# A token-by-token scan: the product of decays moved to GpSimd, one sum reordered, one scaling done a group later

## The chip, the core and the metric

The kernel runs on one core of one Trainium2 chip, in one launch. The metric is the device time of that launch in microseconds (us), read as the median of several runs. A core has five engines with instruction queues of their own: TensorE (PE in the profile), VectorE (DVE), ScalarE (ACT), GpSimd (POOL) and SyncE (SP, which only issues DMAs here). They meet through semaphores: an instruction waits until a counter has reached a value and raises a counter when it is done.

## What is computed

The whole kernel is a stack of four attention-like parts and four feed-forward parts on an input of 8 x 256 x 256. The change touches one part only, the last "attention", which is in truth a recurrence over the 256 tokens of each batch entry (x stands for the normalised input, the context gives the first weights):

```python
lr = 1.0 / X.shape[-1]
def step(W, x_t):
    pre = jnp.einsum('boi,bi->bo', W, x_t)
    y_t = jax.nn.sigmoid(pre)
    dW = jnp.einsum('bo,bi->boi', y_t, x_t) - (y_t ** 2)[..., None] * W
    W_new = W + lr * dW
    return (W_new, y_t)
_, m_traj = lax.scan(step, W_init, jnp.swapaxes(X, 0, 1))
```

Each output row o of W is multiplied at each token by the decay 1 - lr * y_t(o)^2 and gets lr * y_t(o) * x_t added. So pre for a later token s can be carried forward without W: v[s] begins as W_init x_s, and at each token t it becomes v[s] * (1 - lr * y_t^2) + lr * y_t * (x_t . x_s). The inner products x_t . x_s (the "gram") are made ahead of the scan by TensorE.

## The kernel before, in words

`stage_scan` runs `scan_products` (grams and first products), `scan_steps` (the recurrence) and `stage_tail` (the last feed-forward part). The change is in `scan_steps` alone.

A tile holds 128 rows of the output dimension in its partitions and C = 16 columns for (half of the output dimension, batch entry). 256 tokens are walked in NG = 64 groups of TG = 4; four groups make a block of TB = 16. At token t = 4m + i VectorE brings up to date only what lies near: the rest of group m and all of group m + 1. What older groups add to later tokens goes through TensorE, a group at a time: for each group the kernel keeps a = the product of its decays so far (slot 0 of tile `az`) and y of each token, decayed by the tokens behind it in the group (slots 1 to 4). When the group is over, z = y decayed / a (`ra` is the reciprocal of a), TensorE turns z (`ps_z`), ScalarE copies it (`zT`), and TensorE adds its products with the gram to an accumulator in PSUM (`acc`). Two tokens before group m + 1 begins, that accumulator times the running a is the share of all older groups (`far`), and is added to v.

Order of VectorE's queue in one token, with the widths in elements per partition (16 a token):

- `adds` (line 2956): y_t times the gram for the tokens ahead, 48, 96, 80, 64 wide at i = 0, 1, 2, 3.
- `left` for the next token (line 2962): v of it times the decay; the decay comes as nq = -lr * y^2 (line 2971), and (nq + 1) * v is one instruction. 16 wide, 64 at i = 3.
- `az` (line 2962 through 2986 or 2991): a and the y's of this group times the decay, in place, 16, 32, 48, 64 wide.
- v of the next token = `adds` + `left` (line 2993), which waits for `left`. ScalarE waits for this v, makes y by a sigmoid (line 2930), and then a second copy of y for `az` (line 2934).
- `left` for the rest of the tokens ahead, and their sum (line 3036). At i = 0 one more product starts v of the group after (line 2956).
- At i = 2 the rest goes otherwise: `left` (3004), `far` (3008), `left` + `adds` (3012), nq of the next token, and v = `left` + `far` (3017).
- At i = 3: the reciprocal (3025) and z (3030).
- nq of the next token (2971), which waits for ScalarE's y.

ScalarE copies zT of group m - 1 in its queue behind the sigmoids of token 4m + 1 (i = 1), after a wait for TensorE's `z_ps`. TensorE, in each group, waits for z, turns it, does one early piece of work, waits for zT, adds the group's products (which raises `acc_ready`), does a share of products of whole older blocks, and fills up with matmuls on an identity (`ss_idle`, line 3081) until the group has PASSES = 28 passes. GpSimd has no instruction in `scan_steps`.

`step()` in the code raises VectorE's own counter `own`; several waits ahead of one instruction are put on it (the first) and on semaphore instructions ahead of it (the others).

Of the kernel before, what the change touches and what calls it, by code (L numbers as in the profile page):

```python
# [12 lines left out]
P = 128  # L13
# [14 lines left out]
KD = D // P  # L28
# [2843 lines left out]
def scan_steps(nc, core, gd, band, p0, gm, gb, first_in, y_all, LR, TB, TG):  # L2872
# [5 lines left out]
    PASSES = 28  # L2878
    QUARTER = (0, 1, 0, 1, 2, 3, 0, 1, 0, 1, 2, 3, 0, 1, 2, 3)
    with ExitStack() as ctx:  # L2880
        st = Stage(nc, ctx, "ss")
        v = st.sb("v", [P, C, S])
        nq = st.sb("nq", [P, 2, C])
# [3 lines left out]
        az = st.sb("az", [P, 2, C, 1 + TG])  # L2887
# [8 lines left out]
        v_ready, y_ready, yz_ready, z_ready = (st.sem(n) for n in ("v_ready", "y_ready", "yz_ready", "z_ready"))  # L2896
        z_ps, zT_ready, acc_ready, merged = (st.sem(n) for n in ("z_ps", "zT_ready", "acc_ready", "merged"))
# [26 lines left out]
        @block.scalar  # L2924
        def _(act):
            nc.scalar.preload_act_table(ACT.Sigmoid)
            for t in range(S):
                m, i = divmod(t, TG)
                act.wait_ge(v_ready, t + 1)
                nc.scalar.activation(y_all[:, :, :, t], by_batch(v[:, :, t]), ACT.Sigmoid).then_inc(y_ready, 1)  # L2930
                if m < SENT:
                    if i == 0 and m >= 2:
                        act.wait_ge(z_ready, m - 1)
                    nc.scalar.activation(az[:, m % 2, :, 1 + i], v[:, :, t], ACT.Sigmoid).then_inc(yz_ready, 1)
                if i == 1 and 0 < m <= SENT:
                    k, g = divmod(m - 1, PER)
                    rows = slice(32 * g, 32 * (g + 1))
                    act.wait_ge(z_ps, m)
                    nc.scalar.activation(zT[rows, k, :, :].rearrange("p h n -> p (h n)"),
                                         ps_z[(m - 1) % 2][rows, 0:KD * P], ACT.Copy).then_inc(zT_ready, 1)  # L2940

        @block.vector
        def _(dve):
# [16 lines left out]
            def decayed(out, t, src, n):  # L2960

                return nc.vector.scalar_tensor_tensor(  # L2962
                    out, nq[:, t % 2, :].unsqueeze(2).broadcast_to([P, C, n]), 1.0, src, ALU.add, ALU.mult)

            nq_done, summed = {}, [0]

            def square(t):

                yt = y_all[:, :, :, t]
                dve.wait_ge(y_ready, t + 1)  # L2970
                nq_done[t] = step(nc.vector.scalar_tensor_tensor(by_batch(nq[:, t % 2, :]), yt, -LR, yt,
                                                                 ALU.mult, ALU.mult))

            def token(t):
# [9 lines left out]
                if m < NG - 1:  # L2984
                    if i == 0:
                        a_done = step(decayed(az[:, m % 2, :, 0:1], t, az[:, 1 - m % 2, :, 0:1], 1))
                    else:
                        n = 1 + i if m < SENT else 1
                        if n > 1:
                            dve.wait_ge(yz_ready, t)  # L2990
                        a_done = step(decayed(az[:, m % 2, :, 0:n], t, az[:, m % 2, :, 0:n], n))
# [3 lines left out]
                cols = slice(t + 1 + first, t + 1 + old)  # L2995
                if i == 2 and m < NG - 1:
# [7 lines left out]
                    left_done = step(decayed(lft[:, :, first:old], t, v[:, :, cols], old - first))  # L3004
                    if m > 0:
                        dve.wait_ge(acc_ready, m)
                    dve.wait_ge(own, a_done)
                    nc.vector.tensor_tensor(by_batch(far[:, :, :]), past,
                                            by_batch(az[:, m % 2, :, 0:1]).broadcast_to([P, KD, B, TG]), ALU.mult
                                            ).then_inc(merged, 1)  # L3010
                    dve.wait_ge(own, left_done)
                    left_done = step(nc.vector.tensor_tensor(lft[:, :, first:old], lft[:, :, first:old],
                                                             add[:, :, first:old], ALU.add))
                    square(t + 1)
                    dve.wait_ge(merged, m + 1)
                    dve.wait_ge(own, left_done)
                    summed[0] = step(nc.vector.tensor_tensor(v[:, :, cols], lft[:, :, first:old], far[:, :, :], ALU.add))
# [5 lines left out]
                if i == TG - 1 and m < SENT:  # L3023
                    dve.wait_ge(own, a_done)
                    ra_done = step(nc.vector.reciprocal(ra[:, :], az[:, m % 2, :, 0]))
                    dve.wait_ge(own, ra_done)
                    dve.wait_ge(yz_ready, t + 1)
                    if m >= 2:
                        dve.wait_ge(z_ps, m - 1)
                    nc.vector.tensor_tensor(z[:, m % 2, :, :, :].rearrange("p h i b -> p h b i"),  # L3030
                                            by_batch(az[:, m % 2, :, 1:1 + TG]),
                                            by_batch(ra[:, :].unsqueeze(2)).broadcast_to([P, KD, B, TG]), ALU.mult
                                            ).then_inc(z_ready, 1)
# [6 lines left out]
            step(nc.vector.memset(az[:, 1, :, 0:1], 1.0))  # L3040
            nc.vector.tensor_copy(by_batch(v[:, :, 0:TG]), p0[:, :, :, 0:TG]).then_inc(v_ready, 1)
            square(0)
            for t in range(S - 1):
# [6 lines left out]
                token(t)  # L3050

# [422 lines left out]
```

## Time and profile before

| what | value |
| --- | --- |
| median of 3 runs | 2093.52 us (2092.69 to 2096.36) |
| profiled execution, its own time | 2117.26 us |
| its span, first to last instruction | 2115.4 us |
| the scan's tokens in it | about 1741 to 2021 us of the span |
| busy over the whole span: PE, DVE, ACT, POOL | 89%, 60%, 39%, 13% |
| mean granted TensorE clock | 0.942 of full |

The profile is one execution, recorded with every instruction's start and duration in each engine. An instruction of VectorE may start before the one ahead of it has ended, so that sums of durations exceed the time they take; the distance from start to start is what an instruction costs its queue. Idle time ahead of an instruction is shown in brackets with the instruction that ended it.

### The profile page before, as it was taken

The numbers are of one execution on the slowest core, as the hardware profiler recorded it, in microseconds if no ns is written. First come the engines' busy times: TensorE is split into PE (matmuls) and PEld (weight loads), VectorE is DVE, ScalarE is ACT, GpSimd is POOL, SyncE is SP. The second block draws the span as 40 slices with busy tenths as digits, with TensorE's granted clock in tenths as the row PEclk, the third lists the DMA queues.
The fourth block names the chain that finished last, engine by engine and source line by source line (L and its number), as shares of the span: only waits on it lengthen the run. The fifth ranks groups of instructions, "written<-read, shape, count | busy, mean of one in ns | idle before, by whom it ended". The sixth has DMA issues, their size and how long they took to land. (4 is left out here: it accounts for less than half of the span.)

```text
span 2115.4 us, 39004 instructions
## 1 busy us (share of the span) xinstructions
PE 1874.4 (89%) x13651; PEld 1515.8 (72%) x13652; DVE 1270.9 (60%) x4667; ACT 835.4 (39%) x2279; POOL 275.6 (13%) x499
## 2 busy tenths in 40 slices
PE   8799997999998989999999988997940969999978
PEld 6466765667666979999999977775520857777745
DVE  7767764887784351111111144676778518999988
ACT  3333334565563111111111102773477523444468
POOL 2001112000001070000000063430000230000022
PEclk9899998999999999999999998998975987999989
DMA  6111112111112622222222021111000030111101
GB/s 220 65 45 56 55 53 75 41 66 55 41 41 61 237 80 80 82 85 84 82 84 84 25 68 38 48 41 61 0 0 1 0 102 23 35 36 47 25 8 33
DMA packets 106722, 124.95 MB, mean 59 GB/s; under 512 B 36160, under 2 KB 85832, under 8 KB 104776
## 3 DMA queue, kind: packets, MB, share of 16 engines
q1 hardware_dynamic: 95416, 107.25, 15.3%
q0 software_dynamic: 3072, 8.39, 1.3%
q10 hardware_dynamic: 8080, 7.35, 1.1%
q8 instruction: 85, 1.39, 0.3%
q14 instruction: 69, 0.57, 0.1%
HBM read 86.39 MB, written 36.63 MB: 58 GB/s over the span
## 5 line engine op out<-in xcount | busy, mean ns | idle before, releaser
L1762 DVE TENSOR_TENSOR me_h<-me_sg,me_ps_u 128x512 f32<-128x512 f32 x106 | 72.6, 687 | 286.5 <-PE me_ps_u L1585 279.2
L1718 ACT ACTIVATE me_sg<-me_ps_g 128x512 f32<-128x512 f32 x106 | 63.3, 597 | 370.7 <-PE me_ps_g L1585 340.6
L1250 ACT ACTIVATE ca_e<-ca_scored,ca_neg_max 128x256 f32<-128x256 f32 x256 | 127.2, 499 | 108.0 <-DVE ca_neg_max L1309 108.0
L1585 PE MATMUL me_ps_g<-me_x_turned,me_w 128*128 128x128 f32 x1184 | 144.5, 275 | 1.7 <-issue 1.7
L1585 PE MATMUL me_ps_u<-me_x_turned,me_w 128*128 128x128 f32 x1184 | 144.3, 275 | 0.0
L1585 PEld LDWEIGHTS me_ps_g<-me_x_turned,me_w 128*128 128x128 f32 x1184 | 140.7, 192 | 4.2 <-issue 2.5
L1592 PE MATMUL me_ps_y<-me_w,me_h 128*128 128x256 f32 x592 | 140.0, 379 | 0.0
L1585 PEld LDWEIGHTS me_ps_u<-me_x_turned,me_w 128*128 128x128 f32 x1184 | 138.2, 192 | 0.0
L2930 ACT ACTIVATE sc_y_all<-ss_v 128x16 f32<-128x16 f32 x256 | 60.9, 238 | 158.4 <-DVE ss_v L2993 158.3
L1592 PEld LDWEIGHTS me_ps_y<-me_w,me_h 128*128 128x128 f32 x592 | 106.8, 190 | 11.4
L1309 DVE CUSTOM_DVE_ANT_0 ca_scored<-ca_main,ca_mask_add 128x256 f32<-128x256 f32 x256 | 92.8, 418 | 22.3 <-PE ca_main L1190 22.3
L3081 PE MATMUL ss_idle<-ident 128*128 128x128 f32 x648 | 93.2, 292 | 0.0
L2962 DVE SCALAR_TENSOR_TENSOR ss_left<-ss_nq,ss_v 128x16 f32<-128x16 f32 x446 | 90.0, 202 | 0.0
L1964 POOL DMA_INDIRECT me_rows<-moe_y_list,me_slot x32 | 31.2, 975 | 430.6 <-DVE carrier L81 422.4
L3081 PEld LDWEIGHTS ss_idle<-ident 128*128 128x128 f32 x648 | 82.4, 201 | 6.7 <-issue 3.8
L2371 PE MATMUL ig_ps<-nw_int_wT,ig_xT 128*128 128x384 f32 x256 | 86.4, 492 | 0.0
L2168 ACT ACTIVATE la_e<-la_scores,la_mx 128x128 f32<-128x128 f32 x256 | 70.5, 422 | 34.3 <-DVE la_mx L2208 34.3
L1202 PE MATMUL ca_turned<-ident,ca_e 128*128 128x128 f32 x512 | 70.1, 281 | 13.0 <-DVE ca_e L1322 13.0
L1786 DVE COPY me_y<-me_ps_y 128x256 f32<-128x256 f32 x37 | 15.7, 424 | 108.0 <-PE me_ps_y L1592 108.0
L1202 PEld LDWEIGHTS ca_turned<-ident,ca_e 128*128 128x128 f32 x512 | 57.8, 143 | 29.5 <-DVE ca_e L1322 21.8
L1322 DVE TENSOR_SCALAR ca_e<-ca_e,ca_rsums 128x256 f32<-128x256 f32 x256 | 74.5, 354 | 2.2
L1585 PE MATMUL me_ps_g<-me_xT,me_w13s 128*128 128x128 f32 x512 | 67.1, 284 | 6.2 <-issue 5.4
(442 smaller groups left out, 4365.9 us busy)
## 6 DMA issues: line engine op xcount, KB each, us to landing
me_w<-in_L_ffn_w_e SPq DMA_DIRECT2D x24, 1024.0 KB, 7.5
ca_k_list<-kv_out SPq DMA_DIRECT2D x28, 256.0 KB, 2.4
ca_v_list<-kv_out SPq DMA_DIRECT2D x28, 256.0 KB, 2.3
sk_gb<-scan_g_band SPq DMA_DIRECT2D x14, 512.0 KB, 3.7
moe_x_list<-me_zeros SPq DMA_DIRECT2D x1, 5248.0 KB, 21.1
me_x_tile<-moe_x_list SPq DMA_DIRECT2D x38, 128.0 KB, 2.0
moe_y_list<-me_y ACTq DMA_DIRECT2D x37, 128.0 KB, 1.7
ca_kT<-ca_k_list SPq DMA_DIRECT2D x4, 1024.0 KB, 4.8
```

Source lines behind the costliest of these rows:

```text
L1202: last = nc.tensor.transpose(ps[:, jt * S + it * P:jt * S + (it + 1) * P], e[:, g % 3, e_, it, jt * P:(jt + 1) * P], core.ident[:, :])
L1250: nc.scalar.activation(e[:, g % 3, e_, it, :], scored[:, g % 2, e_, it, :], ACT.Exp, scale=-1.0, bias=neg_max[:, g % 2, n:n + 1], accum_ou ...
L1309: last = nc.vector.tensor_tensor_reduce(scored[:, g % 2, e_, it, :], ps[:, it * S:(it + 1) * S], mask_add[:, b, :], -1.0, -NEG, ALU.add, A ...
L1322: last = nc.vector.tensor_scalar(e[:, g % 3, e_, it, :], e[:, g % 3, e_, it, :], rsums[:, par, n:n + 1], None, ALU.mult)
L1585: last = nc.tensor.matmul(ps[:, j * P:(j + 1) * P], w[:, n, kt, f:f + P], x[:, kt, :], start=(kt == 0), stop=(kt == KD - 1))
L1592: last = nc.tensor.matmul(ps_y[:, 0:D], h[:, c, j, :], w[:, f, :], start=(f == 0), stop=(f == FT - 1))
L1718: nc.scalar.activation(sg[:, c, :], ps_g[c][:, :], ACT.Silu).then_inc(done, 1)
L1762: nc.vector.tensor_tensor(h[:, c, :, :].rearrange("p j n -> p (j n)"), sg[:, c, :], ps_u[c][:, :], ALU.mult).then_inc(done[c], 1)
L2168: last = nc.scalar.activation(e[:, n % 2, r, j, :], scores.ps[r][:, j * P:(j + 1) * P], ACT.Exp, bias=mx[:, n % 2, r, j:j + 1])
L2371: last = nc.tensor.matmul(ps[2 * w + c][:, 0:HALF], xT[:, par, kt, :], wT[:, w, kt, c * HALF:(c + 1) * HALF], start=(kt == 0), stop=(kt == ...
L2962: return nc.vector.scalar_tensor_tensor(out, nq[:, t % 2, :].unsqueeze(2).broadcast_to([P, C, n]), 1.0, src, ALU.add, ALU.mult)
L3081: nc.tensor.matmul(idle[:, 0:P], core.ident[:, :], core.ident[:, :], start=True, stop=True)
```

## The change

Four things are changed, all in `scan_steps`:

1. The instructions on `az` leave VectorE. GpSimd does each as two: `lost` = source times nq, and `az` = source + `lost`. `az` has four times the slots (two for the group's parity, two for the token's), `nq` has eight slots in place of two. ScalarE writes its copy of y into the slot that GpSimd reads next.
2. At i = 2 the order is now: v of the next token, `far` = accumulator times a of the tokens through i = 1, `far` + v of the tokens ahead, that sum times the decay (into `left`), nq of the next token, and v = `left` + `adds`. Each of the first three waits for the one ahead of it.
3. The reciprocal and z of group m - 1 move from the end of group m - 1 (i = 3) to the first token of group m: the reciprocal between `left` and v, z behind v.
4. PASSES is 24 in place of 28.

```diff
-    PASSES = 28
+    PASSES = 24
...
-        nq = st.sb("nq", [P, 2, C])
+        NQ = 2 * TG
+        nq = st.sb("nq", [P, NQ, C])
...
-        az = st.sb("az", [P, 2, C, 1 + TG])
+        az, lost = st.sb("az", [P, 2, 2, C, 1 + TG]), st.sb("lost", [P, C, TG])
...
-                    nc.scalar.activation(az[:, m % 2, :, 1 + i], v[:, :, t], ACT.Sigmoid).then_inc(yz_ready, 1)
+                    nc.scalar.activation(az[:, m % 2, i % 2, :, 1 + i], v[:, :, t], ACT.Sigmoid).then_inc(yz_ready, 1)
...
+            def inverse(m):
+                dve.wait_ge(az_done, TG * (m + 1))
+                return step(nc.vector.reciprocal(ra[:, :], az[:, m % 2, 1, :, 0]))
+
+            def scaled(m, ra_done):
+
+                dve.wait_ge(yz_ready, TG * (m + 1))
+                dve.wait_ge(own, ra_done)
+                if m >= 2:
+                    dve.wait_ge(z_ps, m - 1)
+                nc.vector.tensor_tensor(z[:, m % 2, :, :, :].rearrange("p h i b -> p h b i"),
+                                        by_batch(az[:, m % 2, 1, :, 1:1 + TG]),
+                                        by_batch(ra[:, :].unsqueeze(2)).broadcast_to([P, KD, B, TG]), ALU.mult
+                                        ).then_inc(z_ready, 1)
...
-                if m < NG - 1:
-                    if i == 0:
-                        a_done = step(decayed(az[:, m % 2, :, 0:1], t, az[:, 1 - m % 2, :, 0:1], 1))
-                    else:
-                        n = 1 + i if m < SENT else 1
-                        if n > 1:
-                            dve.wait_ge(yz_ready, t)
-                        a_done = step(decayed(az[:, m % 2, :, 0:n], t, az[:, m % 2, :, 0:n], n))
+                if i == 0 and 1 <= m <= SENT:
+                    ra_done = inverse(m - 1)
                 dve.wait_ge(own, left_done)
                 nc.vector.tensor_tensor(v[:, :, t + 1:t + 1 + first], add[:, :, 0:first], lft[:, :, 0:first], ALU.add
                                         ).then_inc(v_ready, 1)
                 cols = slice(t + 1 + first, t + 1 + old)
+                if i == 0 and 1 <= m <= SENT:
+                    scaled(m - 1, ra_done)
                 if i == 2 and m < NG - 1:
...
-                    left_done = step(decayed(lft[:, :, first:old], t, v[:, :, cols], old - first))
-                    if m > 0:
                         dve.wait_ge(acc_ready, m)
-                    dve.wait_ge(own, a_done)
+                    dve.wait_ge(az_done, t)
                     nc.vector.tensor_tensor(by_batch(far[:, :, :]), past,
-                                            by_batch(az[:, m % 2, :, 0:1]).broadcast_to([P, KD, B, TG]), ALU.mult
+                                            by_batch(az[:, m % 2, 1, :, 0:1]).broadcast_to([P, KD, B, TG]), ALU.mult
                                             ).then_inc(merged, 1)
+                    dve.wait_ge(merged, m + 1)
+                    joined = step(nc.vector.tensor_tensor(far[:, :, :], far[:, :, :], v[:, :, cols], ALU.add))
+                    dve.wait_ge(own, joined)
+                    left_done = step(decayed(lft[:, :, first:old], t, far[:, :, :], old - first))
+                    square(t + 1)
                     dve.wait_ge(own, left_done)
-                    left_done = step(nc.vector.tensor_tensor(lft[:, :, first:old], lft[:, :, first:old],
-                                                             add[:, :, first:old], ALU.add))
-                    square(t + 1)
-                    dve.wait_ge(merged, m + 1)
-                    dve.wait_ge(own, left_done)
-                    summed[0] = step(nc.vector.tensor_tensor(v[:, :, cols], lft[:, :, first:old], far[:, :, :], ALU.add))
+                    summed[0] = step(nc.vector.tensor_tensor(v[:, :, cols], lft[:, :, first:old], add[:, :, first:old],
+                                                             ALU.add))
...
-                if i == TG - 1 and m < SENT:
-                    dve.wait_ge(own, a_done)
-                    ra_done = step(nc.vector.reciprocal(ra[:, :], az[:, m % 2, :, 0]))
...
+        @block.gpsimd
+        def _(pool):
+
+
+            nc.gpsimd.memset(az[:, 1, 1, :, 0:1], 1.0).then_inc(az_clear, 1)
+            for t in range(S - TG):
+                m, i = divmod(t, TG)
+                n = 1 + i if m < SENT else 1
+                pool.wait_ge(own, nq_done[t])
+                if t == 0:
+                    pool.wait_ge(az_clear, 1)
+                else:
+                    pool.wait_ge(az_done, t)
+                if i == 0 and m >= 2:
+                    pool.wait_ge(z_ready, min(m - 1, SENT))
+                if n > 1:
+                    pool.wait_ge(yz_ready, t)
+                src = az[:, (m + 1) % 2, 1, :, 0:1] if i == 0 else az[:, m % 2, 1 - i % 2, :, 0:n]
+                nc.gpsimd.tensor_tensor(lost[:, :, 0:n], src, nq[:, t % NQ, :].unsqueeze(2).broadcast_to([P, C, n]),
+                                        ALU.mult).then_inc(lost_ready, 1)
+                pool.wait_ge(lost_ready, t + 1)
+                nc.gpsimd.tensor_tensor(az[:, m % 2, i % 2, :, 0:n], src, lost[:, :, 0:n], ALU.add
+                                        ).then_inc(az_done, 1)
```

## Rows read from the trace of the kernel before

**Rows 1.** Windows of two stretches: length, PE, PEld, DVE, ACT, POOL busy; clock; DMA.

```profile
1741.00:1767.00 26.00, 21.04 (x85) 17.58 (x85) 18.25 (x133) 7.77 (x40) 0.00 (x0) 0.50 0.08 26
1800.00:1900.00 100.00, 92.94 (x661) 76.46 (x660) 98.26 (x731) 42.33 (x212) 0.00 (x0) 1.00 0.14 37
```

**Rows 2.** Timeline of VectorE, four tokens: start, duration, engine, line, operation.

```profile
1852.20 0.18 DVE L2971 SCALAR_TENSOR_TENSOR ss_nq<-sc_y_all 128x16 f32<-128x16 f32 x1
...
1852.64 0.19 DVE L2993 TENSOR_TENSOR ss_v<-ss_adds,ss_left 128x16 f32<-128x16 f32 x1
...
1853.14 0.19 DVE L2971 SCALAR_TENSOR_TENSOR ss_nq<-sc_y_all 128x16 f32<-128x16 f32 x1
...
1853.64 0.19 DVE L2993 TENSOR_TENSOR ss_v<-ss_adds,ss_left 128x16 f32<-128x16 f32 x1
1853.74 0.24 DVE L2962 SCALAR_TENSOR_TENSOR ss_left<-ss_nq,ss_v 128x80 f32<-128x80 f32 x1
1854.01 0.24 DVE L3036 TENSOR_TENSOR ss_v<-ss_adds,ss_left 128x80 f32<-128x80 f32 x1
1854.17 0.18 DVE L2971 SCALAR_TENSOR_TENSOR ss_nq<-sc_y_all 128x16 f32<-128x16 f32 x1
...
1854.65 0.19 DVE L2993 TENSOR_TENSOR ss_v<-ss_adds,ss_left 128x16 f32<-128x16 f32 x1
...
1855.15 0.18 DVE L2971 SCALAR_TENSOR_TENSOR ss_nq<-sc_y_all 128x16 f32<-128x16 f32 x1
1855.35 0.22 DVE L3017 TENSOR_TENSOR ss_v<-ss_left,ss_far 128x64 f32<-128x64 f32 x1
1855.49 0.22 DVE L2956 TENSOR_TENSOR ss_adds<-sk_gb,sc_y_all 128x64 f32<-128x64 f32 x1
...
1855.89 0.22 DVE L2993 TENSOR_TENSOR ss_v<-ss_adds,ss_left 128x64 f32<-128x64 f32 x1
1856.03 0.24 DVE L3025 RECIPROCAL ss_ra<-ss_az 128x16 f32<-128x16 f32 x1
1856.31 0.27 DVE L3030 TENSOR_TENSOR ss_z<-ss_az,ss_ra 128x64 f32<-128x64 f32 x1
1856.45 0.18 DVE L2971 SCALAR_TENSOR_TENSOR ss_nq<-sc_y_all 128x16 f32<-128x16 f32 x1
```

**Rows 3.** Timeline of VectorE near the end of the scan.

```profile
2017.34 0.22 DVE L2962 SCALAR_TENSOR_TENSOR ss_left<-ss_nq,ss_v 128x64 f32<-128x64 f32 x1
...
2017.59 0.22 DVE L2993 TENSOR_TENSOR ss_v<-ss_adds,ss_left 128x64 f32<-128x64 f32 x1
2018.11 0.19 DVE L2971 SCALAR_TENSOR_TENSOR ss_nq<-sc_y_all 128x16 f32<-128x16 f32 x1 [0.30 <-ACT sc_y_all L2930]
...
2018.34 0.19 DVE L2962 SCALAR_TENSOR_TENSOR ss_left<-ss_nq,ss_v 128x16 f32<-128x16 f32 x1
2018.56 0.19 DVE L2993 TENSOR_TENSOR ss_v<-ss_adds,ss_left 128x16 f32<-128x16 f32 x1
```

**Rows 4.** Timeline of all engines around one copy of zT.

```profile
1767.57 0.62 PE L3095 MATMUL ss_ps_z<-ident,ss_z 128*32 128x128 f32 x4
...
1768.23 0.38 ACT L2939 ACTIVATE ss_zT<-ss_ps_z 32x256 f32<-32x256 f32 x1 [1.23 <-PE ss_ps_z L3095]
...
1768.91 0.19 DVE L2971 SCALAR_TENSOR_TENSOR ss_nq<-sc_y_all 128x16 f32<-128x16 f32 x1 [0.88 <-ACT sc_y_all L2930]
```

**Rows 5.** Source view of line 3030: count, duration (min/median/max), first and last start.

```profile
L3030 DVE TENSOR_TENSOR ss_z<-ss_az,ss_ra x62: 266/271/279, 1746.7 to 2013.8; 128x64 f32<-128x64 f32 x62
```

**Rows 6.** Tile views: three kinds of GpSimd arithmetic, one VectorE scaling beside GpSimd.

```profile
L3400 POOL TENSOR_TENSOR bt_up<-bt_cgu,bt_amax x16: 191/192/193, 2027.4 to 2092.5; 128x1 f32<-128x1 f32 x16
...
L2254 POOL TENSOR_TENSOR la_qd<-la_xT,lp_own x32: 606/614/3328, 1306.4 to 1425.1; 128x256 f32<-128x256 f32 x32
...
L182 POOL TENSOR_TENSOR f_ln_rstd<-f_ln_mean_var,eps x16: 191/745/746, 130.6 to 328.6; 128x1 f32<-128x1 f32 x16
...
L1322 DVE TENSOR_SCALAR ca_e<-ca_e,ca_rsums x256: 344/348/811, 348.7 to 659.2; 128x256 f32<-128x256 f32 x128
```

More of the change, by code:

```diff
@@ L2896, in scan_steps @@
         v_ready, y_ready, yz_ready, z_ready = (st.sem(n) for n in ("v_ready", "y_ready", "yz_ready", "z_ready"))
+        az_clear, az_done, lost_ready = st.sem("az_clear"), st.sem("az_done"), st.sem("lost_ready")
+        nq_done = {}
         z_ps, zT_ready, acc_ready, merged = (st.sem(n) for n in ("z_ps", "zT_ready", "acc_ready", "merged"))
@@ L2962, in decayed @@
                 return nc.vector.scalar_tensor_tensor(
-                    out, nq[:, t % 2, :].unsqueeze(2).broadcast_to([P, C, n]), 1.0, src, ALU.add, ALU.mult)
-            nq_done, summed = {}, [0]
+                    out, nq[:, t % NQ, :].unsqueeze(2).broadcast_to([P, C, n]), 1.0, src, ALU.add, ALU.mult)
+            summed = [0]
             def square(t):
@@ L2970, in square @@
                 dve.wait_ge(y_ready, t + 1)
-                nq_done[t] = step(nc.vector.scalar_tensor_tensor(by_batch(nq[:, t % 2, :]), yt, -LR, yt,
+                nq_done[t] = step(nc.vector.scalar_tensor_tensor(by_batch(nq[:, t % NQ, :]), yt, -LR, yt,
                                                                  ALU.mult, ALU.mult))
+            def inverse(m):
[10 more added lines that the diff above has]
+                                        ).then_inc(z_ready, 1)
             def token(t):
@@ L3022, in token @@
                     step(product(v[:, :, TG * (m + 1):TG * (m + 2)], t, TG, 2 * TG))
-                if i == TG - 1 and m < SENT:
-                    dve.wait_ge(own, a_done)
-                    ra_done = step(nc.vector.reciprocal(ra[:, :], az[:, m % 2, :, 0]))
[L3026 to L3033, printed above, removed]
                 if old > first:
@@ L3038, in token @@
                     square(t + 1)
-            step(nc.vector.memset(az[:, 1, :, 0:1], 1.0))
             nc.vector.tensor_copy(by_batch(v[:, :, 0:TG]), p0[:, :, :, 0:TG]).then_inc(v_ready, 1)
```

## The prediction

> **What bounds the kernel now.** I read the page first: the scan is the stretch from about 1741 to 2021 us. The windows view says that there, at full clock, VectorE is busy 98.26 of 100 us, TensorE 92.94, GpSimd not at all [rows 1]. The reader could stop here and say "VectorE is the bound, whatever leaves it is gain". The timeline says something else. In it, four tokens take 1856.45 - 1852.20 = 4.25 us: 0.94, 1.03, 0.98 and 1.30 for i = 0, 1, 2, 3, read from nq to nq [rows 2]. Each token is a chain of four links: nq, `left`, v of the next token, ScalarE's y, and nq again. From `left` to v is 0.22 us (1852.64, where the instruction of `az` stands between them), and near the end of the scan, where nothing stands between them, it is 0.22 too (2018.34 to 2018.56) [rows 2, 3]. So that link is latency: `left` takes 0.18, and v starts 0.04 behind its end. The `az` instruction sits in time that nobody can use. From v to nq is 0.50 us (1852.64 to 1853.14, 1854.65 to 1855.15) [rows 2]; where v is 64 wide and VectorE has nothing else to do it is 0.52, with 0.30 us of idleness put down to ScalarE [rows 3]. So at i = 0 and i = 2 the token is as long as its chain. At i = 1 VectorE's own work is 0.03 longer (0.10 + 0.27 + 0.16 from v to nq), and at i = 3 the reciprocal and z cost 0.04 over the chain (0.56 against 0.52) [rows 2, 3]. VectorE is busy in almost all of the time and yet sets it hardly anywhere: the queue's work and the chain have nearly the same length.
>
> **The change, part by part.** I lay out a new group of four tokens at full clock, times counted from nq of i = 0. A 16-wide instruction costs its queue 0.10 us and a 64-wide one 0.14 [rows 2].
>
> *az leaves VectorE.* At i = 0, 1, 2 it stood in the 0.22 us between `left` and v: worth nothing. At i = 3 `left` to v is 0.25 with a 16-wide instruction between (2017.34 to 2017.59) [rows 3], which is the duration 0.22 of a 64-wide `left` plus 0.03, so it will be 0.25 against 0.27 before.
>
> *i = 0, with the reciprocal and z added.* nq to `left` is 0.22 (0.44 less 0.22). Then `left` 0.10, and the reciprocal: it takes 0.24, and as instructions here cost their queue some 0.085 less than their duration (0.18 against 0.10, 0.22 against 0.14), I take 0.155 [rows 2]. v starts at 0.475. The reciprocal ends at 0.565. z waits for it and, by the code, for two other counters; the wait on `own` is no longer on z itself but on a semaphore instruction ahead of it. The trace has that form once: line 3017 starts 0.20 behind nq, though the 16-wide nq costs 0.10, because of such a wait [rows 2]. I take 0.10 behind the end of the reciprocal: z at 0.665 (with no such cost 0.60). Then z 0.14, `left` 32 wide 0.10, the product 0.14, the sum 0.10: nq of i = 1 at 1.145. The chain alone would give 0.475 + 0.50 = 0.975. So i = 0 costs 0.20 more than the 0.94 of before.
>
> *i = 1, the copy of zT.* v of the next token starts at 1.145 + 0.50 = 1.64; VectorE's own work would give nq at 1.145 + 1.03 = 2.175. But z ends at 0.665 + 0.27 = 0.935, TensorE starts it at about 0.98 and takes 0.62, ScalarE copies zT 0.04 later (1767.57 + 0.62 against 1768.23), at 1.645, and nq follows the start of that copy by 0.68 us (1768.23 to 1768.91), since y of the next token stands behind zT in ScalarE's queue [rows 4]. nq of i = 2 is at 2.325, 0.15 late. Before, z was made 0.8 us earlier and the copy waited for nothing; rows 4 are from the start of the scan, at the change of the clock, and show what the wait does.
>
> *i = 2, far, joined, left.* v is at 0.48 as before (1854.17 to 1854.65), `far` 0.10 behind it, at 0.58. Before, `left`, `far`, and `left` + `adds` followed each other at their queue's cost, and nq at 0.98. Now the sum waits for `far` and `left` for the sum: 0.22 + 0.04 each, so `left` is at 1.10, and nq is behind it in the queue, at 1.23 or 1.24. I take 1.22 to 1.24, call it 1.225: 0.245 late. The four instructions are as many as before; what is new is that they form a chain, and that nq stands behind its end.
>
> *i = 3.* The last sum waits for `left` (ends at 1.32) and starts some 0.12 behind nq, against 0.20 before; then 0.14, 0.14, 0.25, 0.52 [rows 2, 3]: 1.17 against 1.30, a gain of 0.13.
>
> The group takes 2.325 + 1.225 + 1.17 = 4.72 us against 4.25: 0.47 more. Does anything else come late? GpSimd has per token two dependent instructions of 16 to 64 elements. The 1-element one takes 0.192 and the 256-element one 0.614 where nothing disturbs it [rows 6]: 1.65 ns an element, so 0.22, 0.24, 0.27 and 0.30 us. With 0.1 us to see nq and 0.1 between the two the longest token is done 0.19 + 0.1 + 0.30 + 0.1 + 0.30 = 1.0 us behind its nq; the reciprocal asks for it 1.17 + 0.32 behind. It keeps up, with 0.5 us in hand. `acc_ready` needs about 0.4 us of TensorE after zT and after the early piece (2.02, or 2.3 with it), so 2.7, and `far` is at 2.325 + 0.58 = 2.9: hidden, with 0.2 us to spare.
>
> *GpSimd beside VectorE.* The two get in each other's way in this trace, in both directions: a GpSimd addition of one element takes 0.745 in place of 0.191 where a long two-input VectorE instruction runs, and VectorE's scaling, 0.348, takes 0.811 where GpSimd's 256-element additions run [rows 6]. Nearly every VectorE instruction of the scan reads two tiles of SBUF. From below: no delay, as 1-element instructions of GpSimd cause none that I could see. From above: every reading GpSimd does stands in VectorE's chain. 2 x (16 + 32 + 48 + 64) = 320 elements at 1.65 ns are 0.53 us a group. The long operations fall on i = 3, whose `adds`, `left` and v are all on the chain, those of i = 0 and 1 lie partly under the ScalarE delay. I take 0.2.
>
> The Trainium skill, "SBUF — State Buffer", section "Who interferes with whom", says that a VectorE instruction with two SBUF inputs contends with a GpSimd instruction that reads SBUF, under an exclusive lock held for the full instruction, so that the second one blocks fully. By that rule, the trace agrees on blocking; whether short instructions hold it for their full time no row here shows. The rival "held for the whole instruction" below is what this rule would make.
>
> *PASSES.* Four passes fewer take TensorE's filler only. A pass is 92.94 / 661 = 0.14 us, so 24 are 3.4 us of a 4.9 us group, 69% busy where it was 93% [rows 1]. That hides nothing and costs nothing as long as the clock stays at full level.
>
> **Sum.** (0.47 + 0.2) us a group. The z instructions run from 1746.7 to 2013.8 [rows 5], and the clock is at 0.50 until about 1767 [rows 1]; (2013.8 - 1767) / 4.25 = 58 groups. 58 x 0.67 = 39 us, less 1 for the four slow groups at the start, where TensorE was the bound and has four passes less (bounds -3 and +5). +38 us: the profiled execution's 2117.3 becomes 2155, and the median, 24 us below the profiled one, 2093.5 + 38 = 2131. A measurement of this kernel tells about 0.2% (4 us) from no change.
>
> **The rivals.**
> - *Lock for the whole instruction* (0.10). GpSimd's eight operations of a group last 2 x (0.22 + 0.24 + 0.27 + 0.30) = 2.06 us. If VectorE stands for half of it, the group is 4.72 + 1.0 = 5.7: 58 x 1.5 = 85 us, 2178; for all of it, 2240. For it: the 0.811 of rows 6 is the whole of a neighbour's time. Against: the one-element operations seem to block nothing.
> - *The clock stays low* (0.08). In the half-clock stretch VectorE is busy 18.25 of 26 us, at full clock 98.26 of 100, so a group there takes 4.25 x 0.983 / 0.702 = 5.95 us [rows 1]. Each group that stays at 1.2 GHz costs about 1.1 us more; 30 of them give 2131 + 33 = 2164, all of them 2195. For it: TensorE, busy 21.04 of the 26 us before the rise [rows 1], gets less filler. Against: at half clock it would still be nearly full.
> - *VectorE's queue is the bound after all* (0.08), the faster side. Then four `az` instructions are 0.10 + 0.10 + 0.12 + 0.14 = 0.46 us a group, 27 us: 2067. For it: the 98% [rows 1]. It decides if `far`, the sum and `left` overlap instead of waiting, so that nq at i = 2 stays at 0.98, and if z does not hold back ScalarE. Against: the 0.22 of rows 3 with nothing between.
> - *Costs and gains cancel*, within 4 us (0.04): it would need the 0.47 to be a misreading of nearly the whole.
> - *My forecast* (0.70): 2112 to 2152. With no contention 0.47 x 58 = 27, 2120; with all of the 0.53, 1.0 x 58 - 1 = 57, 2150.
>
> **Range.** 2108 to 2175 holds the forecast and the nearer parts of the two slow rivals, about 0.8. Faster 0.08, same 0.04, slower 0.88.
>
> **What would show it.** In the profile after, at full clock: a group of about 4.9 us; `left` to v still 0.22 at i = 1, 2; 0.26 us each between `far`, the sum and `left`; nq 1.2 us behind nq at i = 2; ScalarE's zT waiting for `ps_z` in each group, about 60 times; idle time of VectorE at i = 3. Some two-input VectorE instructions longer than their 0.18 to 0.22 show the contention; if none is, the time is near 2120. Wrong would be: the reciprocal waiting for GpSimd, `far` waiting for `acc_ready`, a clock below full after 1780, or a group under 4.3 us.

## The result, and the profile after

The changed kernel takes 2175.28 us (median of 4 runs, 2172.48 to 2179.97) against 2094.94 for the kernel before: the ratio is 1.0378, with a 95% interval of 1.0359 to 1.0398. It is slower by some 80 us. I forecast slower, by 38 us, and a range that ended at 2175; the measured time is just beyond that end, and twice the forecast's distance.

The profiled executions differ by less than that in their spans, 2172.4 against 2115.4, because the one of before entered the scan some 19 us later (first nq at 1741.5 against 1722.0). The scan itself is what to compare: the first 63 groups last 276.6 us before and 353.0 after, worked out from the starts of ScalarE's y.

The windows view of the changed kernel, in two stretches of 100 us of the scan and two short ones:

```profile
1800.00:1900.00 100.00, 84.22 (x427) 67.85 (x426) 79.42 (x484) 31.88 (x162) 42.47 (x143) 0.72 0.10 25
1900.00:2000.00 100.00, 84.43 (x452) 68.84 (x451) 80.39 (x491) 31.92 (x163) 43.28 (x146) 0.75 0.13 33
1905.00:1911.50 6.50, 4.92 (x36) 3.97 (x34) 5.71 (x36) 2.43 (x12) 3.29 (x11) 1.00 0.31 60
1911.70:1921.70 10.00, 9.56 (x39) 7.62 (x38) 7.70 (x48) 2.72 (x15) 3.96 (x14) 0.50 0.01 2
```

The first two rows answer to the second of [rows 1]. The column to look at is the eighth, the granted clock: 0.72 and 0.75 where it was 1.00. TensorE is busy 84 us where it was 93, with 427 matmul records where there were 661, so it gets through fewer matmuls in nearly as much busy time. The two short rows show what the mean hides: 6.5 us at full clock, with TensorE busy 4.92 of 6.50 (76%), and then 10 us at half clock, with TensorE busy 96%. The clock goes up and down all through the scan; in sum it is at half for 197 of the 355 us.

Timeline of the changed kernel over four tokens, nearly all of it at full clock (the rows of GpSimd and ScalarE that matter with VectorE's):

```profile
1904.71 0.19 DVE L2974 SCALAR_TENSOR_TENSOR ss_nq<-sc_y_all 128x16 f32<-128x16 f32 x1
...
1905.20 0.19 DVE L3005 TENSOR_TENSOR ss_v<-ss_adds,ss_left 128x16 f32<-128x16 f32 x1
1905.30 0.38 ACT L2942 ACTIVATE ss_zT<-ss_ps_z 32x256 f32<-32x256 f32 x1 [0.73 <-PE ss_ps_z L3120]
...
1905.97 0.19 DVE L2974 SCALAR_TENSOR_TENSOR ss_nq<-sc_y_all 128x16 f32<-128x16 f32 x1 [0.15 <-ACT sc_y_all L2933]
...
1906.45 0.19 DVE L3005 TENSOR_TENSOR ss_v<-ss_adds,ss_left 128x16 f32<-128x16 f32 x1
...
1906.58 0.22 DVE L3020 TENSOR_TENSOR ss_far<-ss_acc,ss_az 128x64 f32<-128x64 f32 x1
...
1906.84 0.23 DVE L3024 TENSOR_TENSOR ss_far<-ss_far,ss_v 128x64 f32<-128x64 f32 x1
...
1907.10 0.23 DVE L2965 SCALAR_TENSOR_TENSOR ss_left<-ss_nq,ss_far 128x64 f32<-128x64 f32 x1
1907.24 0.18 DVE L2974 SCALAR_TENSOR_TENSOR ss_nq<-sc_y_all 128x16 f32<-128x16 f32 x1
...
1907.51 0.37 POOL L3071 TENSOR_TENSOR ss_lost<-ss_az,ss_nq 128x64 f32<-128x64 f32 x1 [0.58 <-DVE ss_nq L2974]
1907.64 0.32 DVE L2965 SCALAR_TENSOR_TENSOR ss_left<-ss_nq,ss_v 128x64 f32<-128x64 f32 x1
1907.96 0.31 POOL L3074 TENSOR_TENSOR ss_az<-ss_az,ss_lost 128x64 f32<-128x64 f32 x1
1907.99 0.36 DVE L3005 TENSOR_TENSOR ss_v<-ss_adds,ss_left 128x64 f32<-128x64 f32 x1
...
1908.65 0.19 DVE L2974 SCALAR_TENSOR_TENSOR ss_nq<-sc_y_all 128x16 f32<-128x16 f32 x1 [0.30 <-ACT sc_y_all L2933]
...
1908.98 0.25 DVE L2979 RECIPROCAL ss_ra<-ss_az 128x16 f32<-128x16 f32 x1
1909.14 0.15 DVE L3005 TENSOR_TENSOR ss_v<-ss_adds,ss_left 128x16 f32<-128x16 f32 x1
...
1909.32 0.29 DVE L2987 TENSOR_TENSOR ss_z<-ss_az,ss_ra 128x64 f32<-128x64 f32 x1
...
1909.83 0.18 DVE L2974 SCALAR_TENSOR_TENSOR ss_nq<-sc_y_all 128x16 f32<-128x16 f32 x1
```

This answers to [rows 2]. nq stands at 1904.71 (i = 1), 1905.97, 1907.24, 1908.65 (i = 0 of the next group) and 1909.83. At i = 2 `far`, its sum with v and `left` start 0.26 us from each other, each on the end of the one ahead, and nq is 1.27 behind nq. At i = 3 a 64-wide `left` takes 0.32 and v 0.36, where both took 0.22. `left` started while GpSimd's `lost` ran, 1907.51 to 1907.88, and ended at 1907.96; v started while GpSimd's `az` ran, 1907.96 to 1908.27, and ended at 1908.35: both times 0.08 behind the end of GpSimd's instruction. The z of i = 0 starts 0.09 behind the end of the reciprocal.

Timeline of the same kernel in a half-clock stretch:

```profile
1852.92 1.06 PE L3120 MATMUL ss_ps_z<-ident,ss_z 128*32 128x128 f32 x4 [0.64 <-DVE ss_z L2987]
...
1854.03 0.37 ACT L2942 ACTIVATE ss_zT<-ss_ps_z 32x256 f32<-32x256 f32 x1 [1.09 <-PE ss_ps_z L3120]
1854.42 0.23 ACT L2933 ACTIVATE sc_y_all<-ss_v 128x16 f32<-128x16 f32 x1
...
1854.69 0.19 DVE L2974 SCALAR_TENSOR_TENSOR ss_nq<-sc_y_all 128x16 f32<-128x16 f32 x1 [0.51 <-ACT sc_y_all L2933]
...
1856.33 0.22 DVE L3020 TENSOR_TENSOR ss_far<-ss_acc,ss_az 128x64 f32<-128x64 f32 x1 [0.97 <-PE ss_acc L3097]
```

TensorE turns z in 1.06 us in place of 0.62. ScalarE waits 1.09 us for it and copies zT, the next y starts only behind that copy, VectorE stands 0.51 us ahead of nq, and then 0.97 ahead of `far`, because TensorE's products come late too. This is how TensorE's clock gets into the chain.

The waits view of the changed kernel, from 1741 to 2100 us (total, times, longest):

```profile
ACT ss_zT L2942 <- PE ss_ps_z L3120: 54.7, 60, 2.1
...
DVE ss_nq L2974 <- ACT sc_y_all L2933: 36.0, 95, 1.5
DVE ss_far L3020 <- PE ss_acc L3097: 16.8, 19, 1.0
```

ScalarE waits for `ps_z` in every group, as forecast. The last two lines are VectorE's real losses, and both are long only where the clock is low. In stretches wholly at full clock nq never waited longer than 0.30 us, as in the timeline above at 1908.65, and `far` is not among the waits at all.

### The profile page after: what moved, and what is told of

Same layout as the page of the kernel before. It is cut to its first block and busy times, and to the rows that moved or that the text cites. A ratio compares the mean times of both kernels' runs of the same rounds, so it can differ in the third digit from the quotient of the medians.

```text
span 2172.4 us, 38965 instructions
## 1 busy us (share of the span) xinstructions
PE 1900.7 (87%) x13399; PEld 1536.9 (71%) x13424; DVE 1286.7 (59%) x4414; ACT 833.0 (38%) x2279; POOL 424.9 (20%) x1004
## 5 line engine op out<-in xcount | busy, mean ns | idle before, releaser
L3071 POOL TENSOR_TENSOR ss_lost<-ss_az,ss_nq 128x16 f32<-128x16 f32 x252 | 76.8, 305 | 184.3 <-DVE ss_nq L2974 184.3
L3120 PE MATMUL ss_ps_z<-ident,ss_z 128*32 128x128 f32 x248 | 53.3, 355 | 57.1 <-DVE ss_z L2987 56.0
L3106 PE MATMUL ss_idle<-ident 128*128 128x128 f32 x420 | 88.7, 372 | 0.0
L3106 PEld LDWEIGHTS ss_idle<-ident 128*128 128x128 f32 x420 | 76.1, 268 | 9.4 <-issue 8.0
L2965 DVE SCALAR_TENSOR_TENSOR ss_left<-ss_nq,ss_v 128x16 f32<-128x16 f32 x383 | 81.6, 213 | 0.1
L3088 PE MATMUL ss_acc<-sk_gm,ss_zT 128*128 128x128 f32 x420 | 81.4, 344 | 0.0
L3120 PEld LDWEIGHTS ss_ps_z<-ident,ss_z 128*32 128x32 f32 x248 | 28.3, 137 | 75.0 <-DVE ss_z L2987 71.8
```

The costliest lines, as they stand in the source:

```text
L2965: return nc.vector.scalar_tensor_tensor(out, nq[:, t % NQ, :].unsqueeze(2).broadcast_to([P, C, n]), 1.0, src, ALU.add, ALU.mult)
L3071: nc.gpsimd.tensor_tensor(lost[:, :, 0:n], src, nq[:, t % NQ, :].unsqueeze(2).broadcast_to([P, C, n]), ALU.mult).then_inc(lost_ready, 1)
L3088: nc.tensor.matmul(acc[n % 2][:, h, 0:P], zT[:, k, h, :], gm[:, gram_pair(n, k), :, :].rearrange("p b t -> p (b t)"), start=False, stop=Tr ...
L3106: nc.tensor.matmul(idle[:, 0:P], core.ident[:, :], core.ident[:, :], start=True, stop=True)
L3120: last = nc.tensor.matmul(ps_z[m % 2][rows, h * P:(h + 1) * P], z[:, m % 2, h, :, :].rearrange("p i b -> p (i b)"), core.ident[:, :], star ...
```

## The experiments

All times are medians of interleaved runs against the kernel before on the same chip, with the ratio and its 95% interval; the kernel before came out at 2093.1 to 2094.9 from one set of runs to the next, and its row has one of them. "Group" is the median length of a group that lies wholly at full clock, "low" the time at half clock in the scan of the profiled execution; both are worked out from the starts and the clock in the traces.

| kernel | time, us | ratio (interval) | group, us | low, us |
| --- | --- | --- | --- | --- |
| before | 2094.3 | | 4.25 | 26 |
| changed | 2175.3 | 1.0378 (1.0359 to 1.0398) | 4.97 | 197 |
| after_p28 | 2148.9 | 1.0255 (1.0237 to 1.0274) | 5.00 | 74 |
| after_p32 | 2143.8 | 1.0226 (1.0206 to 1.0246) | 5.02 | 30 |
| after_p36 | 2145.8 | 1.0254 (1.0237 to 1.0272) | 5.02 | 16 |
| after_p32_zt | 2181.8 | 1.0429 (1.0412 to 1.0447) | 5.52 | 78 |
| before_p24 | 2096.2 | 1.0010 (0.9996 to 1.0023) | 4.25 | 29 |
| before_p20 | 2130.5 | 1.0181 (1.0164 to 1.0198) | 4.25 | 194 |
| before_order | 2117.2 | 1.0100 (1.0083 to 1.0117) | 4.55 | 26 |
| before_order2 | 2109.6 | 1.0088 (1.0064 to 1.0112) | 4.42 | 22 |
| before_z | 2120.8 | 1.0126 (1.0109 to 1.0142) | 4.66 | 26 |
| before_both | 2132.8 | 1.0188 (1.0171 to 1.0205) | 4.88 | 16 |
| before_pool | 2118.3 | 1.0109 (1.0092 to 1.0126) | 4.60 | 36 |
| before_warm | 2091.7 | 0.9990 (0.9980 to 1.0000) | 4.24 | 2 |

The same groups by token, from nq to nq, medians:

| kernel | i = 0 | i = 1 | i = 2 | i = 3 |
| --- | --- | --- | --- | --- |
| before | 0.94 | 1.03 | 0.98 | 1.30 |
| forecast, without contention | 1.145 | 1.18 | 1.225 | 1.17 |
| after_p32 | 1.18 | 1.17 | 1.27 | 1.42 |
| before_order | 0.94 | 1.03 | 1.35 | 1.23 |
| before_order2 | 0.94 | 1.03 | 1.23 | 1.23 |
| before_z | 1.25 | 1.17 | 0.98 | 1.26 |
| before_pool | 0.96 | 1.06 | 1.06 | 1.52 |
| before_both | 1.25 | 1.17 | 1.27 | 1.19 |
| after_p32_zt | 1.18 | 1.02 | 1.90 | 1.42 |

### Is it the clock? Filler in the changed kernel

```diff
# after_p28, after_p32, after_p36: the changed kernel with
-    PASSES = 24
+    PASSES = 28      # 32, 36
```

> The changed kernel with PASSES back at 28. Theory 1, two parts: at full clock the group is 4.97 us against 4.25 (45 us in 63 groups), and the rest of the 80 us is TensorE's clock, which falls again and again since TensorE is busy only some 70% of a group, and which then holds ScalarE's copy of zT and VectorE's far. With four passes more TensorE is busy 28 x 0.14 = 3.9 of 4.97 us, 79%: fewer falls or none, groups of 4.97, time 2138 to 2155. Rival 2: the clock is not on the chain and the whole is contention and order: time stays at 2175, within 4 us.

> The changed kernel with PASSES 32, TensorE busy 4.5 of 4.97 us, 90%. Theory 1: clock at full level from the first groups on, every group 4.97 us, 2094.9 + 63 x 0.72 = 2140, within 5. Rival 2: 2175 or, since TensorE then gets to z later, more. A third reading, that TensorE's longer work itself holds z back, would show as TensorE busy when z is ready, and groups over 5.1 at full clock.

> The changed kernel with PASSES 36: 36 x 0.14 = 5.0 us of filler and work in a group of 5.0. If more filler than keeps the clock up is free, 2140 to 2144; if TensorE comes late to z, each group gets longer by what it is late, up to 0.2 us: up to 2157. It tells on which side of 32 the best is.

Windows of after_p28, and below it of after_p32:

```profile
1800.00:1900.00 100.00, 84.25 (x550) 71.44 (x548) 86.37 (x529) 34.93 (x178) 46.48 (x156) 0.91 0.12 31
1900.00:2000.00 100.00, 85.40 (x541) 72.46 (x541) 85.04 (x519) 34.15 (x174) 46.01 (x154) 0.88 0.14 33
```

```profile
1800.00:1900.00 100.00, 87.71 (x628) 75.22 (x628) 86.63 (x531) 34.52 (x175) 46.59 (x157) 0.97 0.12 31
1900.00:2000.00 100.00, 87.65 (x638) 75.11 (x636) 87.31 (x534) 35.22 (x178) 47.32 (x159) 0.98 0.14 33
```

Nothing but filler was added to TensorE, and the kernel became 26 us faster with four passes a group and 31 us with eight. The granted clock goes from 0.72 to 0.91 and 0.97. With 36 passes the time at half clock is down to 16 us and the total no better: the intervals of 32 and 36 overlap. The reading that the clock lies beside the chain is out. The group at full clock stays at 5.0 us in all of them, so 47 us of the 80 (2.26% of 2094) are not the clock's. The other 31 to 33 are. VectorE's wait ahead of nq in after_p32 shows where they went, against 36.0 us in 95 waits in the changed kernel; `far` waited once, for 1.0 us, against 19 times:

```profile
DVE ss_nq L2974 <- ACT sc_y_all L2933: 22.2, 65, 0.9
```

### Is less filler enough by itself? Filler in the kernel before

```diff
# before_p24, before_p20: the kernel before with
-    PASSES = 28
+    PASSES = 24      # 20
```

> The kernel before with PASSES 24 alone, TensorE busy 3.4 of 4.25 us, 79%. Theory 1: if the clock falls in some stretches, each low group costs 1 to 2 us, 2100 to 2130; if 79% is enough to keep it, within 4 us of the kernel before, less 1 to 3 us for shorter groups in the half-clock stretch at the start. Rival 2: no difference whatever the clock does.

> The kernel before with PASSES 20 alone. Nothing of GpSimd, of the order or of z is changed; TensorE is busy about 20 x 0.14 = 2.8 of 4.25 us, 66%, less than the 70% of the changed kernel. Clock theory: the granted clock falls again and again as in the changed kernel, and low groups are 1.2 to 2 us longer: 2105 to 2135. Rival: the falls of the changed kernel come from the long waits of the new order, not from the share of filler; then the clock stays and the time is 2094 within 4 us.

Windows of before_p24, and below it two of before_p20:

```profile
1800.00:1900.00 100.00, 82.64 (x568) 66.23 (x567) 98.30 (x730) 42.23 (x211) 0.00 (x0) 1.00 0.15 38
```

```profile
1800.00:1900.00 100.00, 91.81 (x418) 71.70 (x416) 88.05 (x639) 36.61 (x184) 0.00 (x0) 0.65 0.13 36
1900.00:2000.00 100.00, 89.55 (x464) 72.39 (x464) 84.85 (x620) 36.09 (x180) 0.00 (x0) 0.74 0.14 33
```

The four passes that the change took away cost the kernel before nothing: TensorE is busy 82.64 of 100 us and the clock stays at 1.00. Four more, and the clock is 0.65 and 0.74, 194 us of the scan are at half clock, and the time is 37 us longer, with no instruction of VectorE, ScalarE or GpSimd changed and the group at full clock still 4.25. So neither the long waits of the new order nor GpSimd is needed for the clock to fall; less filler in a group is enough. It lies with the group's length as much as with PASSES: 24 passes in 4.25 us hold the clock, 24 passes in 4.97 us do not, and 28 in 5.0 us hold it for most of the time only. The Trainium skill, "TensorE: Matmul & The Clock Gate", Part 1, says that a monitor sets the clock by how busy the array has recently been; by that rule, these runs agree.

### The order at i = 2

```diff
# before_order: the kernel before, az of i = 2 not ahead of v but behind far
-                if m < NG - 1:
+                if m < NG - 1 and i != 2:
...
-                    left_done = step(decayed(lft[:, :, first:old], t, v[:, :, cols], old - first))
...
                     nc.vector.tensor_tensor(by_batch(far[:, :, :]), past,
...
                     dve.wait_ge(merged, m + 1)
+                    a_last[0] = step(decayed(az[:, m % 2, :, 0:n], t, az[:, m % 2, :, 0:n], n))
+                    joined = step(nc.vector.tensor_tensor(far[:, :, :], far[:, :, :], v[:, :, cols], ALU.add))
+                    dve.wait_ge(own, joined)
+                    left_done = step(decayed(lft[:, :, first:old], t, far[:, :, :], old - first))
+                    square(t + 1)
+                    dve.wait_ge(own, left_done)
+                    summed[0] = step(nc.vector.tensor_tensor(v[:, :, cols], lft[:, :, first:old], add[:, :, first:old],
+                                                             ALU.add))
# before_order2: the line of a_last stands behind the line of joined
```

> The kernel before with the order of i = 2 alone: far from a of the tokens through i = 1, az decayed behind far, far + v, left, nq, v. az, the reciprocal and z stay on VectorE and at their place, PASSES 28. By the chain as I read it nq at i = 2 comes 0.245 us late and 0.07 of it comes back at i = 3: 0.17 x 63 = 11 us, 2106. Rival: VectorE's queue is the bound and the count of its instructions is the same, so 2095 within 4 us.

> As before_order, but the az instruction of i = 2 stands behind the sum far + v, not ahead of it. In before_order the sum started 0.38 us behind far, since az waited for far too and then took 0.13 of the queue; behind the sum az fits into the 0.26 us that the next left waits anyway. Chain theory: 0.12 x 63 = 8 us less than before_order, near 2109, a group of 4.43. Rival, the count of VectorE's instructions decides: no change, 2117.

before_order came out 23 us slower, twice what I expected: i = 2 took 1.35. My own edit had put `az` into the chain, between `far` and the sum. With `az` behind the sum, i = 2 is 1.23 and i = 3 is 1.23, +0.25 and -0.07, the two numbers of the chain. Timeline of before_order2, VectorE:

```profile
1850.75 0.19 DVE L2971 SCALAR_TENSOR_TENSOR ss_nq<-sc_y_all 128x16 f32<-128x16 f32 x1
...
1851.33 0.22 DVE L3008 TENSOR_TENSOR ss_far<-ss_acc,ss_az 128x64 f32<-128x64 f32 x1
1851.58 0.23 DVE L3012 TENSOR_TENSOR ss_far<-ss_far,ss_v 128x64 f32<-128x64 f32 x1
1851.73 0.20 DVE L2962 SCALAR_TENSOR_TENSOR ss_az<-ss_nq,ss_az 128x48 f32<-128x48 f32 x1
1851.85 0.23 DVE L2962 SCALAR_TENSOR_TENSOR ss_left<-ss_nq,ss_far 128x64 f32<-128x64 f32 x1
1851.98 0.19 DVE L2971 SCALAR_TENSOR_TENSOR ss_nq<-sc_y_all 128x16 f32<-128x16 f32 x1
1852.10 0.22 DVE L3021 TENSOR_TENSOR ss_v<-ss_left,ss_adds 128x64 f32<-128x64 f32 x1
```

`far` 1851.33, the sum 1851.58, `left` 1851.85, nq 1851.98: 0.25, 0.27, 0.13. The count of VectorE's instructions is that of before, and the total 16 us longer, with an interval of 13 to 23 (63 groups by 0.17 would be 11).

### The reciprocal and z one token later

```diff
# before_z: the kernel before; in token(), between left and v
+                if i == 0 and 1 <= m <= SENT:
+                    dve.wait_ge(own, a_last[0])
+                    ra_done = step(nc.vector.reciprocal(ra[:, :], az[:, (m - 1) % 2, :, 0]))
# and behind v the z of group m - 1, with waits for yz_ready, ra_done and z_ps;
# the same two are taken out at i = TG - 1
```

> The kernel before with the reciprocal and z moved alone to the first token of the next group, as in the change; az stays on VectorE, at i = 0 too. Chain theory: i = 0 is 0.20 to 0.30 longer (reciprocal, wait, z), i = 1 up to 0.15 longer by ScalarE's copy of zT waiting for ps_z, i = 3 shorter by 0.04 only. Group 4.6 to 4.7, 2117 to 2122. Rival, the queue's work is only moved: 2095 within 4 us.

i = 0 is 0.31 longer, i = 1 0.14, i = 3 0.04 shorter: 0.41 a group, 27 us. The waits view of before_z, where GpSimd does nothing:

```profile
ACT ss_zT L2939 <- PE ss_ps_z L3098: 41.3, 60, 1.5
DVE ss_nq L2971 <- ACT sc_y_all L2930: 21.0, 64, 0.9
```

ScalarE waits for `ps_z` in 60 groups, and VectorE behind it. To see how much of i = 1 is that wait, the copy of zT was moved:

```diff
# after_p32_zt: the changed kernel, PASSES 32
-                if i == 1 and 0 < m <= SENT:
+                if i == 2 and 0 < m <= SENT:
```

> The changed kernel with PASSES 32 and ScalarE's copy of zT one token later, behind the sigmoids of i = 2. ScalarE then waits for no ps_z ahead of a y, and i = 1 loses up to 0.15 us; but TensorE's products and acc_ready come later by about 0.3, and far at i = 2 waits for them. If the wait for ps_z is worth what I say, y(4m+1) to y(4m+2) falls from 1.40 to about 1.25, and the wait comes back at far: total 2138 to 2148. Rival, the 0.41 of i = 1 is the queue's (reciprocal and z) alone: y(4m+1) to y(4m+2) stays at 1.40, far waits on top, over 2148.

i = 1 fell from 1.17 to 1.02, the 0.15 of the chain, which makes that wait ScalarE's and not the queue's. But i = 2 rose from 1.27 to 1.90, far more than the 0.3 that I had expected, and the kernel is 38 us slower than after_p32, outside the 2138 to 2148 that I expected. Most of it is the group, 5.52 against 5.02; the longer group also has the clock at half for 78 us where after_p32 had 30, with the same 32 passes. The waits view:

```profile
DVE ss_far L3020 <- PE ss_acc L3097: 39.5, 55, 2.4
...
DVE ss_nq L2974 <- ACT sc_y_all L2933: 16.7, 55, 0.3
```

`far` now waits in 55 groups for TensorE, whose products of the group follow zT. z made a token later has no slack at either place tried here: it was paid at i = 1 or at i = 2.

### GpSimd beside VectorE

```diff
# before_pool: the kernel before, and on tiles of GpSimd's own (daz, dlost, dnq)
+        @block.gpsimd
+        def _(pool):
...
+            for t in range(S - TG):
+                m, i = divmod(t, TG)
+                n = 1 + i if m < SENT else 1
+                pool.wait_ge(own, nq_done[t])
+                pool.wait_ge(dummy, 2 + 2 * t)
+                src = daz[:, 1 - i % 2, :, 0:n]
+                nc.gpsimd.tensor_tensor(dlost[:, :, 0:n], src, dnq[:, :].unsqueeze(2).broadcast_to([P, C, n]),
+                                        ALU.mult).then_inc(dummy, 1)
+                pool.wait_ge(dummy, 3 + 2 * t)
+                nc.gpsimd.tensor_tensor(daz[:, i % 2, :, 0:n], src, dlost[:, :, 0:n], ALU.add
+                                        ).then_inc(dummy, 1)
```

> The kernel before, unchanged on all other engines, with GpSimd doing on tiles of its own, which nobody reads, two operations a token of the same shapes and at the same times as in the changed kernel. The output is the reference's. It prices contention alone. In the changed kernel the 64-wide left and v at i = 3 take 0.32 and 0.36 us where they took 0.22: 0.24 a group, so here 15 to 25 us, 2110 to 2120. Rival, the port is held for the whole of each GpSimd instruction: 1 to 2 us a group, 2157 or more. Rival, no contention: 2095.

Nobody reads what GpSimd makes, and the kernel is 24.8 us slower, at the upper end of what I expected and far from the 63 us or more of a lock that costs VectorE every instruction of GpSimd. Groups of VectorE by shape in before_pool (count, busy, mean ns):

```profile
L2965 DVE SCALAR_TENSOR_TENSOR ss_az<-ss_nq,ss_az 128x64 f32<-128x64 f32 x57 | 18.8, 331 | 0.0
L2959 DVE TENSOR_TENSOR ss_adds<-sk_gb,sc_y_all 128x64 f32<-128x64 f32 x57 | 18.2, 320 | 0.2 <-issue 0.2
```

Both take 0.22 in the kernel before, and there is one of each at i = 3: 0.11 and 0.10 us more. Four more are longer in the same view: `az` of 48, 32 and 16 elements (0.28, 0.25 and 0.22 against 0.20, 0.19 and 0.18) and the product that starts v of the group after (0.27 against 0.22). GpSimd is busy some 2.4 us a group in the changed kernel (eight operations of 0.24 to 0.37), and work of the same shapes cost VectorE 0.35 here. The Trainium skill, "SBUF — State Buffer", section "SBUF: two separate sides", has whichever of the two starts first hold the shared ports for its whole instruction while the other blocks. By that rule, the timeline of the changed kernel agrees: the two blocked instructions ended 0.08 us behind the end of GpSimd's. What the rule does not tell is how often it bites. In after_p32 only `left` and v of i = 3 are clearly longer than in the kernel before (0.32 and 0.36 against 0.22). Why the others escape is not shown; my reading is that they start ahead of GpSimd's instruction, or in time in which VectorE's chain waits anyway.

### Do the parts add up?

```diff
# before_both: the edits of before_order2 and before_z together, PASSES 32, az on VectorE
```

> The kernel before with the order of i = 2 (as before_order2) and the moved reciprocal and z (as before_z) together, PASSES 32, az still on VectorE. If the two add up, a group of 4.25 + 0.18 + 0.41 = 4.84, some 2093.5 + 63 x 0.59 = 2131 less what overlaps; the difference to after_p32 (2144, 5.01 us) is then what GpSimd costs net, 0.17 a group. Rival, az on GpSimd is a gain that the order and z hide: before_both slower than after_p32.

The group is 4.88 (4.84 expected) and the time 2132.8, 39.7 us over before; after_p32 is 2143.8, 5.02. So az on GpSimd costs about 8 to 11 us net at equal clock. By token: i = 0 is 0.07 shorter on GpSimd, since `az` no longer stands with the reciprocal between `left` and v, and i = 3 is 0.23 longer, which is the blocked `left` and v (0.10 and 0.14).

### A warm clock at the start

```diff
# before_warm: the kernel before
             start_block(0)
             start_block(1)
+            busy(20)
```

> The kernel before with ten more filler matmuls for TensorE at the start of the scan, in the 5 us in which it waits for the first z. The clock was at half until 1767 us and the first four groups took 24.4 us in place of 17. If the filler lets the clock rise some 10 to 15 us earlier, 2 to 7 us are saved: 2088 to 2092. Rival: the clock rises no earlier, since only the denser filler of later groups brings it up, 2094 within 2 us.

In the profiled execution the half-clock stretch is over 2 us into the scan, and the first 63 groups take 268.9 us in place of 276.6. The median is only 1.9 us lower and the interval reaches 1.000. It is the only version here with a lower median than the kernel before (before_p24 could not be told from it either), and whether it is faster this does not settle.

## Why the prediction was off, point by point

- **What bounds the kernel.** Right. VectorE was busy 98% and not the bound: taking its four `az` instructions away gained 0.07 us at i = 0 and nothing at i = 1 and i = 2, as can be read from after_p32 against before_both. In after_p32 98% became 87%, and the group is longer.
- **The chain terms.** i = 0 and i = 1 together 2.325 forecast, 2.34 to 2.35 measured; i = 2 1.225, measured 1.27 (1.23 in before_order2); the 0.2 us to spare that I gave `acc_ready` was not there: at full clock `far` starts 0.61 us behind nq in the middle group of after_p32 and 0.69 in some, against 0.58 in all of before_order2, and before_both, without GpSimd, has 0.61 too; i = 3 1.17, measured 1.42, and 1.19 where GpSimd does nothing (before_both).
- **Contention.** 0.2 a group taken; i = 3 is 0.23 longer in after_p32 than in before_both. In before_pool, where VectorE still has `az` in its queue, i = 3 is 0.22 longer and the whole group 0.35. The group at full clock was forecast as 4.92 and is 4.97 to 5.02.
- **The clock: the step that failed.** "Four passes fewer take TensorE's filler only. [...] That hides nothing and costs nothing as long as the clock stays at full level." I worked out that TensorE would be busy 69% of a group, against 93%, and put the clock at full level without a row that showed it holding at 69%. It did not: 197 us of the scan ran at 1.2 GHz, and after_p32 puts the price at 31 to 33 us. This was the rival "the clock stays low", which I gave 0.08, and "a clock below full after 1780" was on my own list of what would be wrong. It came in part, and as an oscillation: in the stretches shown TensorE was busy 76% of the time ahead of a fall and 96% ahead of the next rise. I had its price per low group too small as well: 1.1 us forecast, 6.36 - 4.97 = 1.39 measured over 20 groups wholly at half clock.
- **My reason against it**, that at half clock TensorE would be nearly full, is true and beside the point: it says that the clock rises, not that it stays.
- **The range.** It ended at 2175 as it held only the nearer parts of the two slow rivals, the lock and the clock. Without the clock, after_p32 is the kernel that I forecast, and it takes 2144 against 2131: 6 us are groups of 5.02 in place of 4.92, two or three more the groups that I left out of the 58 and took as 1 us shorter: the scan's total is 46.1 us longer (322.7 against 276.6), where 58 groups of 0.77 make 44.7. The other 4 or 5 are about what this measurement leaves open. That 2175 was missed by so little is luck: in the sum the clock stood at nothing.
- **The faster rival** (VectorE's queue as the bound) is out: before_order2 and before_z keep VectorE's work the same and cost 16 and 27 us.

## What to carry to other kernels

An engine that is busy 98% need not be the bound: look for an instruction that waits on its neighbour's result, and for a place in the trace where the instruction in question is missing and the distance is the same. Filler matmuls are part of the time budget: a change that makes the group longer thins them out even if their count stays, so where a change touches them or the group's length, expect the clock to move unless a row shows it held under the same conditions, and run the change with more filler too. Work moved to GpSimd costs VectorE the remainder of each GpSimd instruction that it runs into, so place it where VectorE's chain waits for another engine.

## What the runs showed that I had not expected

The kernel before lost nothing with 24 passes a group (granted clock 1.00) and 37 us with 20 (0.65 and 0.74, 194 us at half clock): four filler passes decide over 1.8% of the time in a kernel whose TensorE does nothing on the chain but turn z and add a group's products. Where the wait for the reciprocal stands on a semaphore instruction of its own, z starts 0.09 us behind the reciprocal's end (the changed kernel, after_p32, before_z, before_both); where it stands on z itself, 0.03 to 0.04 (the kernel before, before_order2, before_pool): 0.05 to 0.06 us for the form of the wait, with or without GpSimd at work. GpSimd's first operation of a token (`lost`) took 0.24, 0.30, 0.31 and 0.37 us for 16, 32, 48 and 64 elements a partition, and its second (`az`) 0.25, 0.31, 0.29 and 0.31, for the most part above the 0.22 to 0.30 that I had drawn from 1 and 256 elements.
